# Two adaLN blocks on one core: in wide attention VectorE does the background's ticks of a place ahead of the row maximum of the unit two ahead

## The reference, cut to what matters

```
# layer 0, attention: 16 heads of 16, the 32 largest scores of a row
scores = where(causal, -inf, q @ k.T / sqrt(16))
vals, idx = top_k(scores, 32)
attn = softmax(scores where kept, else -inf);  y = (attn @ v) @ Wo.T + bo
# layer 1, attention: 16 heads of 64, plain causal softmax
scores = Q @ K.T / sqrt(64) + triu(-10000, k=1)
probs = softmax(scores);  vals = probs @ V;  y = vals @ W_out + b_out
```

## Time and profile before

| what | value |
|---|---|
| time, median of 3 runs | 6225.56 us (6222.17 to 6227.89) |
| time of the profiled execution | 6224.38 us |
| its span, first to last instruction | 6222.7 us |
| mean granted clock of TensorE | 0.88 |
| busy share | TensorE 80%, VectorE 67%, ScalarE 45%, GpSimd 29% |
| HBM traffic | 25 GB/s over the span |

### The profile page before, as it was taken

One profiled execution on the slowest core, in us unless ns is written; L12 is line 12 of the kernel. 1 busy time (PEld: TensorE's weight loads), 2 busy tenths in 40 slices (PEclk: granted clock), 3 DMA queues, 4 the chain that ended last, 5 costly groups with the idle time before them and its releaser, 6 DMA issues. The chain is left out here.

```text
span 6222.7 us, 84570 instructions
## 1 busy us (share of the span) xinstructions
PE 4986.2 (80%) x31689; PEld 3196.3 (51%) x31689; DVE 4198.5 (67%) x8611; ACT 2791.2 (45%) x5885; POOL 1775.7 (29%) x1429
## 2 busy tenths in 40 slices
PE   4444478888678988888678988889777998997789
PEld 2333345566335655666434654656534664665256
DVE  5999866777886856777786856668787755224511
ACT  2443315664354524656254633656344542553321
POOL 2565502333233401333232421334322430001000
PEclk7566689999789989999798998999888998998899
DMA  2000000000100110000201010000100010001000
GB/s 99 11 11 24 1 29 22 14 17 10 47 30 31 35 53 24 12 12 14 55 17 38 28 67 20 12 12 17 41 30 21 26 39 24 10 15 33 28 28 34
DMA packets 75086, 169.70 MB, mean 27 GB/s; under 512 B 15176, under 2 KB 36528, under 8 KB 71352
## 3 DMA queue, kind: packets, MB, share of 16 engines
q1 hardware_dynamic: 72632, 163.77, 8.3%
q10 hardware_dynamic: 2048, 0.53, 0.0%
HBM read 130.92 MB, written 26.26 MB: 25 GB/s over the span
## 5 line engine op out<-in xcount | busy, mean ns | idle before, releaser
L1373 DVE MAX8 vals<-work 128x8 f32<-128x128 f32 (+7 forms) x1536 | 1081.7, 745 | 0.6
L1718 POOL TENSOR_SCALAR keep<-ssb,vals 128x128 bf16<-128x128 f32 (+7 forms) x512 | 875.1, 1721 | 0.0
L1705 POOL TENSOR_TENSOR pool_step<-ones 128x2 f32<-128x2 f32 x256 | 49.5, 193 | 2536.4 <-DVE vals L1373 2536.2
L428 PE MATMUL ring<-ident,pr 128*128 128x128 f32 x2304 | 470.1, 323 | 360.4 <-POOL pr L1723 329.5
L1387 DVE MATCH_REPLACE8 work<-vals,work 128x128 f32<-128x128 f32 (+7 forms) x1024 | 751.5, 741 | 0.0
L535 PE MATMUL pA<-SC 128*128 128x512 f32 (+3 forms) x1536 | 626.7, 518 | 131.1 <-ACT SC L1116 109.6
L1723 POOL TENSOR_TENSOR pr<-keep,pr 128x128 f32<-128x128 bf16 (+7 forms) x512 | 647.2, 1285 | 0.0
L1055 ACT ACTIVATE prT<-ring 128x512 f32<-128x512 f32 (+1 forms) x768 | 379.4, 495 | 566.0 <-PE ring L428 564.8
L1502 DVE TENSOR_REDUCE nmax<-pA 128x1 f32<-128x1024 f32 (+7 forms) x512 | 382.7, 751 | 317.1 <-PE pA L536 306.0
L428 PEld LDWEIGHTS ring<-ident,pr 128*128 128x128 f32 x2304 | 326.4, 165 | 496.1 <-POOL pr L1723 355.3
L723 PE MATMUL pA<-hT,SC 128*128 128x512 f32 x1024 | 494.6, 606 | 0.0
(11 more groups left out here) (198 smaller groups left out, 8581.6 us busy)
## 6 DMA issues: line engine op xcount, KB each, us to landing
SC<-in_w SPq DMA_DIRECT2D x64, 512.0 KB, 4.4
parts<-SC SPq DMA_DIRECT2D x72, 256.0 KB, 2.4
SC<-in_wqkv SPq DMA_DIRECT2D x32, 384.0 KB, 2.9
stage<-parts SPq DMA_DIRECT2D x64, 192.0 KB
SC<-parts SPq DMA_DIRECT2D x24, 384.0 KB
stage<-parts SPq DMA_DIRECT2D x64, 128.0 KB
SC<-in_ffn_we SPq DMA_DIRECT2D x4, 2048.0 KB, 10.8
SC<-in_wqkv SPq DMA_DIRECT2D x8, 768.0 KB, 7.6
```

Source lines behind the costliest of these rows:

```text
L428: mm = pe.transpose(r[:, blk % 4 * P:blk % 4 * P + P], pr0[:, p % 2, blk * P:blk * P + P], ident[:, :])
L1373: m = v.max(vals0[:, y, i, 8 * n:8 * n + 8], src[:, lo:hi])
L1718: pool.tensor_scalar(keep0[:, lo:hi], ssb0[:, p % 2, lo:hi], vals0[:, p % 2, i, TOPK - 1:TOPK], None, ALU.is_ge).then_inc(s["k"], 1)
```

## The change

In VectorE's program of the wide stage the two statements at a place change their order: first the ticks of place u, then the row maximum of unit u+2. Nothing is added or removed, and no other engine's program changes.

```diff
                     rowmax(G, 0)
                     rowmax(G, 1)
                     for u in range(16):
+                        at("wide", g * 17 + 1 + u)
                         if u + 2 < 16:
                             rowmax(G, u + 2)
-                        at("wide", g * 17 + 1 + u)
                 inverse(b * 8 + 7)
```

## The result

The changed kernel takes 6311.55 us (median of 4 runs, 6303.87 to 6317.15), the kernel before 6224.97 in the same comparison. The ratio is 1.0138 (95% interval 1.0121 to 1.0156): 87 us slower. The forecast was 6263 in a range of 6215 to 6300. Its sign was right, its size was not: 38 us were forecast. The rival "The stalls carry" gave 6311.

The account below looks back on a forecast made before the run. The bound was taken to change within a group between VectorE and a chain through TensorE or ScalarE. An item loses 13.3 - 3.7 + 3 = 12.6 us, three items 38, giving 6263 us, range 6215 to 6300.

Parts of the forecast that it names:

- The stalls carry: Rival: the middle's 2.4 us stalls are not caught, 19 us an item and not 3; 6311 us, chance 0.14.
- What bounds the kernel: Wide stage: the bound changes within a group between VectorE and the chain through TensorE or ScalarE; one chain at its end.
- The gain at the start of a group: Ticks of places 0 and 1 fill 2.7 us of VectorE's idle time, paying for the phase shift, no more.
- The loss at the end: Places 12 and 13: tick 0 waits for copy 6 ahead of a row maximum; 1.9 us in seven groups, 13.3 an item.
- The gain in group 4: Place 12: tick 6 precedes row maximum 14, so GpSimd's select starts earlier; 3.7 us taken, between nothing and 4.4.
- the middle: Middle of a group: tick 0 delays row maximum 5, its exponential 2.4 us late; 3 us an item taken from 0 to 19.
- the catch: Ahead of exponential 10 ScalarE stood 2.26 us for a narrow product, so a maximum late by that much costs nothing there.
- VectorE's rate is the bound: Rival: filling 2.7 us idle at 24 group starts gains 65 us, less 14 at the ends; 6175 us, chance 0.13.
- Slack takes it: Rival: slack behind the row maxima or TensorE's pace absorbs the delay, no change; 6226 us, chance 0.13.
- The order of one queue: VectorE is strict FIFO, so a MAX8 waiting for ScalarE holds the row maximum behind it even when its scores are ready.
- the alternative: VectorE could pass a waiting MAX8: the two losses would be nothing, the sum near group 4's gain, 11 us faster.

Follow-up runs that it names:

- e5: Changed kernel, but a background block's first MAX8 and replacement read rows of X, so tick 0 needs no wait for ScalarE's copy; 6193.94 us, ratio 0.9941.
- e6: Kernel before (old order) with the same reads of X and no wait for the copy, control of e5; 6224.89 us, ratio 0.9994.
- e4: Kernel before with the new order at places 12 and 13 alone, the ends of groups; 6255.30 us, ratio 1.0044.
- e3: Kernel before with the new order at places 0 to 11 alone; 6279.87 us, ratio 1.0083.
- e10: Changed kernel with the background's score pieces and their copies made two ticks earlier on TensorE and ScalarE; 6176.34 us, ratio 0.9918 to the kernel before.
- e12: Kernel before (old order) with the background's score pieces and copies made two ticks earlier, control of e10; 6213.55 us, ratio 0.9976.
- e8: Changed kernel with VectorE's ticks two late, except ahead of each group's first row maximum; 6275.41 us, ratio 1.0068 to the kernel before.
- e14: As e8, but VectorE's ticks are two late ahead of each group's first row maximum too; 6217.08 us, ratio 0.9983 to the kernel before.
- e1: Kernel before with the new order everywhere, but ticks ahead of a row maximum stop short of a tick 0; 6294.18 us, ratio 1.0111.
- e2: Kernel before with the new order only at places whose ticks contain a tick 0; 6329.64 us, ratio 1.0161.

## Why the prediction had the sign and not the size

**What bounds the kernel** was right. The waits moved as the last part of the prediction said: copy 6 above 20 us (48.2), the scores to about half (51.0 to 19.2), the maxima above 41.2 (75.3), item 3's stage unchanged (386.9 us). The stage was to grow by 9 to 17 us and grew by 32 to 34.

**The gain at the start of a group** pays for the phase and no more: right in the changed kernel, where exponential 4 of groups 0 and 1 starts within 0.01 us of its old place. It pays no more once the copy is not late: groups 0 and 1 of e5 are 0.3 and 0.1 us shorter than those of e6.

**The loss at the end** was right: 9.6 us an item against 10.2 in e4. Group 4 is 3.0 us shorter in e4's item 0 (82.06 to 79.07), where 3.7 were taken, which leaves (10.2 + 3.0) / 7 = 1.9 us for each other group, as taken. In the changed kernel the ends of groups 0 and 1 add 2.8 to 2.9, as the delayed middle makes copy 6 later than the old time that was assumed. **The gain in group 4** was right in its mechanism too: 3.8 to 4.5 us with the copy's wait away (e5).

**The step that failed** is that of the middle: "I take the carried part between 0 and 2.4 us a group, 0 to 19 us an item, and choose 3 us, near the row that shows the catch." The mechanism was named and its raw size was nearly right (2.4 forecast, 2.9 measured at exponential 5). What was wrong is the catch, and with it the choice within the bounds: 55.2 / 3 = 18.4 us an item were carried. The upper bound was not one either, since it prices a single tick 0 for the middle of a group. A group holds 222 / 8 = 27.8 ticks, so about four of its ticks are a tick 0, and more than one of them lies in the middle; in e3's item 0 two a group, 15 in all, waited there, 25.9 us together. (18.4 - 3) x 3 = 46 us is nearly the whole miss of 49 us. The earlier trace rows show ScalarE idle for 2.26 us, and I read that as slack against a late maximum. But that copy waits for TensorE, whose products come behind transposes of the delayed exponentials. When the loop shifts, the wait shifts with it, and it was 2.26 us again. Only an event that does not hang on the delayed chain can absorb a stall. For the copy itself the same question was not asked: copy 6 of the next block stands behind the delayed exponentials, so the next tick 0 meets a late copy and not the old one.

**The rivals.** "The stalls carry" (0.14) is what happened: 3 x (9.6 + 19) = 86 us against 86.6. That its price fits so well is partly luck, for it is made of one stall of 2.4 us a group carried whole, and what the runs show is two of 1.7 us a group, of which 18.4 of 25.9 us are carried. "VectorE's rate is the bound" had its condition right, "once copy 6 is ready before VectorE gets to tick 0": with it met, the order gives 31 us (e5 against e6) or 37 us (e10 against e12), where 51 were worked out. Its mechanism did not come true: the starts of groups 0 and 1 gained almost nothing, and the gain within the stages is mostly that of group 4. That e10's 6176 lies beside the 6175 of that rival is chance, and 15 us of it are the copies' own. "Slack takes it" is excluded by e3 and e4.

**The order of one queue** held as the prediction cited it from the Trainium skill, "Perfetto Trace Analysis", section "Tensor Engine Instruction": in group 1 maximum 5 starts at 1034.71, behind the MAX8 that waited until 1032.63. By the alternative the sum would have come out faster, and it did not.

## What to carry to other kernels

Where an operation that waits is put ahead of a critical one on an in-order queue, follow what it waits for back through the other engines: if it hangs on the critical operation of a round earlier, each stall comes round again, and an idle stretch on that same loop catches nothing. Make the awaited work earlier first, and change the order then; here the same order was worth 87 us lost with the copy just in time and 37 us won with it two ticks earlier. When part of such a change is tried alone, look at the spacing of the critical operations before reading the time, for ticks that pile up ahead of one of them cost by themselves: e8, which catches up two ticks ahead of the first maximum of each group, is 56 us slower than e14, which does not, each taken against its own kernel before. In e1 and e2 such a piling up is likely and was not tested.

## What the hardware showed unexpectedly

A tiny operation of VectorE had no fixed duration. The negation of two numbers a partition in the changed kernel's stage of item 0, from the groups of VectorE (busy us, mean ns, idle before):

```profile
L1380 DVE TENSOR_SCALAR nmx<-vals 128x2 f32<-128x2 f32 x31 | 17.6, 568 | 1.1
```

In the kernel before it was 13.0 us, 418 ns in the mean. Single ones last 0.17 us (983.13 in e10), 0.81 in the rows above (991.72), and up to 2.12 us in this stage. The five above 0.9 us all run beside the multiplications at the end of GpSimd's `select` (L1723); the two that ran with GpSimd idle took 0.17 us. But nearly all of the 31 run beside some part of `select`, and some of those take 0.17 us too. That the two engines get in each other's way was not tested by itself, and it is 4.6 us of a stage's 32.
